# A fused three-block kernel: the end of the weight fold reordered, and the expert rows cleared earlier in the transfer queue

## The reference, cut to what matters

```python
x = x + xattn(layernorm(x), ctx)     # latent cross-attention to 257 context rows, 16 heads
x = x + attn(layernorm(x))           # 4-bit-coded weights w = codes * scales, 16 heads of 128
x = x + ffn(layernorm(x))            # 64 experts, top 8 of each token, capacity 128

q_big  = einsum('bshk,hkq->bshq', hidden @ Wq.T, w_kc_q)
kv_rope = kv * cos + rotate_half(kv) * sin
scores = einsum('bhsr,bhlr->bhsl', q_big @ W_qr, kv_rope @ W_kr)
out    = (softmax(scores) @ kv_rope @ w_kc_kv) @ Wo.T
```

## Time and profile before

| | us |
|---|---|
| median of three runs (lowest, highest) | 736.1 (734.83, 737.74) |
| the profiled execution | 734.79 |
| its span, first to last instruction | 733.0 |
| PE busy | 631.6 (86%) |
| DVE busy | 446.3 (61%) |
| ACT busy | 285.6 (39%) |
| POOL busy | 275.1 (38%) |
| fold | to about 84 |
| tile 0, tile 1 | about 84 to 132, about 132 to 187 |

### The profile page before, as it was taken

How to read it: one execution, slowest core, us unless ns; L and a number is a source line. 1 busy time by engine, 2 the same in 40 slices (tenths; PEclk the granted TensorE clock), 3 DMA queues, 4 the chain that set the end, 5 groups by cost and what they waited for, 6 DMA issues and landing times.

```text
span 733.0 us, 16840 instructions
## 1 busy us (share of the span) xinstructions
PE 631.6 (86%) x6395; PEld 540.9 (74%) x6395; DVE 446.3 (61%) x1257; ACT 285.6 (39%) x788; POOL 275.1 (38%) x296
## 2 busy tenths in 40 slices
PE   5998687989989999999999999998886899999900
PEld 3887556977887896896897896896765688778800
DVE  1143696555677577677677677576573245555548
ACT  1112485336337337337347337346030043333300
POOL 3852599211212612612612612403103435555520
PEclk9556798999999999999999999999999999999965
DMA  7697551990400600500500200100002769998467
GB/s 192 191 250 185 164 190 35 293 325 4 138 2 2 199 2 9 193 2 10 192 3 10 77 3 10 56 3 31 32 4 86 203 196 334 330 318 277 131 254 296
DMA packets 90383, 95.85 MB, mean 131 GB/s; under 512 B 26047, under 2 KB 82104, under 8 KB 89280
## 3 DMA queue, kind: packets, MB, share of 16 engines
q1 hardware_dynamic: 83552, 78.40, 35.8%
q0 software_dynamic: 6144, 15.96, 6.0%
q10 hardware_dynamic: 608, 0.42, 0.2%
HBM read 60.19 MB, written 36.18 MB: 131 GB/s over the span
## 4 chain that ended last, share of the span: by engine, by line
PE 52%; DVE 17%; issue 11%; ACT 8%; DMA 4%; SPq 4%; POOL 2%; another core or an unknown queue 1%; POOLq 0%; DVEq 0%; ACTq 0%
PE bank L1258 6%; PE bank L1259 6%; PE bank L1260 6%; PE bank L1324 4%; PE bank L1292 3%; PE bank L1373 3%; PE bank L1278 3%; PE bank L1543 3%; PE bank L1313 3%; DMA Wh<-expert_rows 2%; POOL pair_rows L650 2%; ACT diag L735 2%; PE bank L1511 2%; ACT qspace L676 2%; DVE space L1212 2%
## 5 line engine op out<-in xcount | busy, mean ns | idle before, releaser
L697 ACT ACTIVATE pr<-bank,nmax 128x257 f32<-128x257 f32 x128 | 61.4, 480 | 95.5 <-DVE nmax L921 92.5
L574 POOL DMA_INDIRECT expert_rows<-h,slot x64 | 63.0, 984 | 69.4 <-DVE slot L1018 53.7
L1258 PE MATMUL bank<-space,Wh 128*128 128x128 f16 x512 | 88.1, 219 | 0.3
L1260 PE MATMUL bank<-space,Wl 128*128 128x128 f16 x512 | 88.1, 219 | 0.0
L1259 PE MATMUL bank<-space,Wh 128*128 128x128 f16 x512 | 88.1, 219 | 0.0
L557 POOL TENSOR_TENSOR Cr<-C,Ct 128x192 f32<-128x192 f32 x64 | 39.3, 636 | 122.4 <-PE bank L1324 113.3
L650 POOL DMA_INDIRECT pair_rows<-Wh,etok x64 | 62.4, 974 | 56.5 <-issue 36.2
L921 DVE TENSOR_REDUCE nmax<-bank 128x1 f32<-128x257 f32 x128 | 53.4, 421 | 43.0 <-PE bank L1306 30.1
L705 ACT COPY pT<-bank 128x256 f32<-128x256 f32 x128 | 47.6, 372 | 64.1 <-PE bank L1313 61.5
L1324 PE MATMUL bank<-Cr,pT 128*128 128x64 f32 x512 | 72.2, 264 | 0.1
L1324 PEld LDWEIGHTS bank<-Cr,pT 128*128 128x128 f32 x512 | 68.2, 194 | 0.2 <-ACT pT L705 0.2
(11 more groups left out here) (208 smaller groups left out, 1548.2 us busy)
## 6 DMA issues: line engine op xcount, KB each, us to landing
expert_rows<-h SPq DMA_DIRECT2D x8, 1120.0 KB, 13.3
Wh<-expert_rows SPq DMA_DIRECT2D x64, 140.0 KB
pair_rows<-zrow SPq DMA_DIRECT2D x8, 1024.0 KB
Wl<-L_ffn_gate_up_proj_dram SPq DMA_DIRECT2D x36, 192.0 KB
ring<-L_ffn_gate_up_proj_dram SPq DMA_DIRECT2D x28, 192.0 KB
space<-pair_rows SPq DMA_DIRECT2D x5, 1024.0 KB, 9.2
Wl<-L_ffn_down_proj_dram SPq DMA_DIRECT2D x36, 96.0 KB
C<-ctx_dram SPq DMA_DIRECT2D x24, 128.0 KB
```

The source lines that it names most:

```text
L574: e.indirect_dma_start(XE[:, :], bass.IndirectOffsetOnAxis(ap=slot[:, k:k + 1], axis=0), h3[:, :], None, bounds_check=E * CAP - 1, oob_is_ ...
L697: e.activation(pr[:, s, :], bank[r % 2][:, 0:NL], ACT.Exp, bias=nmax[:, s:s + 1], accum_out=rsum[:, s:s + 1]).then_inc(expd, 1)
L1258: e.matmul(dst, ah, bh, start=first and n == 0, stop=False)
L1260: ins = e.matmul(dst, al, bh, start=False, stop=last and n == len(terms) - 1)
```

## The change

`FOLD_PARTS` goes from (0, 0, 2, 3) to (0, 0, 1, 4): part 0 alone stays in the third group, and parts 1 to 4 are given to the fourth. Part 4's multiply and cast are done in tile 0 at r = 1. DVE takes part 1 ahead of `kt0`'s low half, part 2 ahead of `qa`'s, part 3 behind `fQ`, and the split of the value bias ahead of the last `M` copy. PE makes `qb` at r = 2 of tile 0, so behind the first two score rows. POOL does the rope products of tile 1 in the fold, between the low halves of parts 0 and 1, and SP loads context 1 ahead of part 1. SP issues the eight `blank` transfers ahead of the wait for all parts; transfer n waits for `expd` 6 + 2n, that is for 6, 8, ... 20 rows.

```diff
-FOLD_PARTS = (0, 0, 2, 3)
+FOLD_PARTS = (0, 0, 1, 4)
@@ SP
             load_fold_first(3)
+            e.wait_ge(roped, 2 * BT)
+            load_context(1)
             load_part(1)
...
                 load_codes(LATE + n, late[n], late_in[n])
-            e.wait_ge(roped, 2 * BT)
-            load_context(1)
-
             e.wait_ge(f_m, GROUPS)
...
             load_codes(PARTS - 1, late[10], late_in[10])
-            e.wait_ge(w_done, PARTS)
...
+            e.wait_ge(iotas, 2)
+            for n in range(E // 8):
+                e.wait_ge(expd, 6 + 2 * n)
+                blank(n)
+
+            e.wait_ge(w_done, PARTS)
             for n in range(NB):
                 load_expert(n, n)
             for i in range(2, T):
                 e.wait_ge(roped, i * (2 * BT))
                 load_context(i)
-                if i == 2:
-                    e.wait_ge(iotas, 2)
-                    for n in range(E // 8):
-                        blank(n)
@@ POOL
-            for u in range(PART0[GROUPS]):
+            part_low(0)
+            rope_products(1)
+            for u in range(1, PART0[GROUPS]):
                 part_low(u)
...
-                if not last:
+                if not last and i != 0:
                     rope_products(i + 1)
@@ ACT, in tile 0 behind exp_row; and in the fold
+                        if isinstance(i, int) and i == 0 and r == 1:
+                            x_use(XNEXT[-1], 0)
+                            part_high(LATE - 1)
...
-                for u in range(PART0[g], PART0[g + 1]):
+                for u in range(PART0[g], min(PART0[g + 1], LATE - 1)):
                     part_high(u)
-
-            x_use(XNEXT[-1], 0)
@@ DVE, in tile 0 behind max_row; and in the fold
+                        if isinstance(i, int) and i == 0 and r == 1:
+                            part_mul(LATE - 1)
+                            x_low(XNEXT[-1], 0)
...
                 if g == GROUPS - 1:
-                    for name in XNEXT[1:-1]:
-                        x_low(name, 0)
-                if len(left) > 2:
                     part_mul(left.pop(0))
+                    x_low("kt0", 0)
+                    part_mul(left.pop(0))
+                    x_low("qa", 0)
@@ PE, in tile 0 ahead of score_row
+                        if isinstance(i, int) and i == 0 and r == 2:
+                            e.wait_ge(f_md, GROUPS)
+                            e.wait_ge(f_na, GROUPS)
+                            x_use("qb", 0)
                         if r < ROWS:
                             score_row(i, r)
...
-            e.wait_ge(f_md, GROUPS)
-            e.wait_ge(f_na, GROUPS)
-            x_use("qb", 0)
             tile(0, None, None)
```

More of the change, by code:

```diff
@@ L1146, in _ @@
                     part_mul(left.pop(0))
+                if g == GROUPS - 1:
+                    e.wait_ge(rwT_ready, 3)
+                    e.tensor_copy(bvh[:, :], bvT[:, :]).then_inc(bv_split, 1)
+                    e.wait_ge(bv_split, 1)
+                    e.tensor_tensor(bvl[:, :], bvT[:, :], bvh[:, :], ALU.subtract).then_inc(bv_split, 1)
                 e.wait_ge(f_m, g + 1)
@@ L1152, in _ @@
                     next_h1(0)
-                for u in left:
-                    part_mul(u)
-            x_low(XNEXT[-1], 0)
+                if g < GROUPS - 1:
+                    for u in left:
+                        part_mul(u)
             e.sem_inc(h3_free, FREE)
             e.wait_ge(iotas, 2)
[L1160 to L1163, removed]
             tile(0, None, None)
```

## The result

The changed kernel takes 746.58 us (median of 4 runs) against 735.47 us for the kernel before, 11.1 us more, a ratio of 1.0152 with a 95% interval of 1.0102 to 1.0203. On a second chip it was 1.0201 (1.0160 to 1.0241), 741.04 us against 727.94. The forecast was 745.8, slower. The profiled execution took 746.07, with a span of 744.3, which is 11.3 more than the span before.

What follows compares the result with a forecast made beforehand. PE carries half the chain and fills tile 1, though no engine holds it everywhere. +0.7 + 11.8 + 2.0 - 4.8 = +9.7 on 734.8 gave 744.5, or 745.8 as median; range 740.5 to 752.

Steps and rivals of the forecast that it cites:

- The context behind the clearing: Tile 1, SP's queue: context 2 waits behind clearing transfers 6 and 7 and 16 expert issues, reaching POOL at 154.7.
- DVE's wait and PE's loss: Tile 1: DVE stands from 145.9 to 159.2, PE loses 11.8 us, and its lowered clock adds 2.0.
- What may come back: Middle of tile 1: PE's unexplained wait and the low clock behind it vanish, -4.8 us; the other end is 0.
- The 3.14: PE's wait in us before 163.89 in tile 1, with no releaser, read as a late instruction refill behind clearing traffic.
- the rival at 750.5: Tile 1: the 3.14 stays, or a like one comes to tile 0; +14.5, 750.6 us; chance 0.28.
- The fold's end: Up to row 2 of tile 0: waiting for part 4's load replaces the shortened path, +0.7 us (+0.1 to +1.5).
- my bracket for row 2: Tile 0: score row 2 starts at 88.7, between 88.1 and 89.5, by the landing of part 4's scales.
- no wait: Fold, DVE: part 3, landed by 75.8, is multiplied at about 76 without waiting.
- The bias split: Fold, DVE: its two small operations move into the wait for M, hidden, and 0.4 us at most otherwise.

Runs made afterwards that it cites:

- context_ahead_of_last_two: The changed kernel with context 2 loaded between the sixth and seventh clearing transfers; 735.36 us against 738.17 for the kernel before, 0.9984.
- clearing_and_context_alone: The kernel before, old fold, with clearing ahead of the wait for all parts and context 2 between its sixth and seventh transfers; 733.72 us against 736.82, 0.9951.
- clearing_only: The kernel before with only the eight clearing transfers moved ahead of the wait for all parts, with their row waits; 753.6 us against 738.17, 1.018.
- order_only: The changed kernel with the clearing put back behind context 2, where it was before; 739.05 us against 738.17 for the kernel before, 1.0011.

## Why the prediction was right

The direction, the mechanism and its place were right. The sum was near, +9.7 forecast and +11.1 measured on the first chip, but that nearness is partly luck: the stages add up to +13.4, as worked out below, and the second chip had +13.1. The steps, by the stages:

*The context behind the clearing: right, with terms that partly cancel.* The gate opened at 137.2, 6.5 behind the first maximum of tile 1, as before. The last clearing transfer issued in 0.36 where I had 0.75. The 16 expert transfers took 11.07 (137.75 to 148.82) where I had 8.82. That is the term I sized too low: I took the issue time ahead of the clearing, and here two clearing transfers were still in front, with the first four issues at 0.56 to 1.31 and a later one at 1.35. The other kernels bear it out: the 16 issues took 7.7 to 9.0 in the three that issue them ahead of the clearing, and 10.8 to 12.5 in the eight that issue them right behind two clearing transfers. The landing was quicker, 3.06 behind the last issue (150.35 to 153.41) instead of 3.78. Altogether POOL had the context 22.7 behind the first maximum of tile 1, and I had 21.4 (154.7 less 133.3).

*DVE's wait and PE's loss.* DVE waited 14.5 where I had 13.3, and PE 11.9 where its loss was to be 11.8 in all. With the half clock that followed the stage grew from 53.2 to 68.2, 15.0; I had 11.8 + 2.0 = 13.8. PE's clock came back in some 5 us, as in the earlier trace rows.

*What may come back: the size right, its nature not shown.* The 3.14 was a wait under the clearing traffic, and it went also in the kernels where PE has no long pause that could hide it (context_ahead_of_last_two, 0.5 at that matmul). With its clock it is worth 57.6 - 53.2 = 4.4; I had 4.8. That it is a fetch of instructions I infer from "issue" and the traffic; what the runs show is that the wait needs the clearing's traffic at that matmul. Here the Trainium skill's page "Runtime: NRT & Kernel Launch", section "Instruction fetch mechanics", with its "mostly hidden", was the rival at 750.5 (750.6 by the forecast's own terms). It didn't come about. The page does say "mostly", and of all waits without a releaser that PE has in tile 1 only this one followed the traffic.

*The fold's end: the place right, the size too small.* I said that a wait for part 4's load would take the place of the path that was shortened, at +0.7. That wait is 4.42, 4.45, 6.14 and 3.32 in four of the five traces with the changed kernel's fold; in the fifth, context_ahead_of_last_two, it is 0.59, and `qb` is the later one. With full clock row 2 stands 29.5, 29.4, 30.4 and 28.5 behind the third M copy in the new order, mean 29.4, and 26.5 and 26.6 in the old: +2.8. With half clock it is 30.8 against 29.1 and 29.4: +1.6. By the same mark my bracket for row 2, 88.1 to 89.5, was 26.6 to 28.0. That row 2 started at 86.07, ahead of the bracket, is due to the early third M copy alone. `part_low(1)` took 2.93 instead of 2.12, and the last scales were in DVE's hands 6.0 behind their issue at 77.4, where the longest landing in the earlier trace rows was 5.4. The codes of parts 5 and 6 were issued right behind them. I didn't test which of these it was. Part 3, for which I had written "no wait", waited 1.04 for its scales, and 0.78 to 1.98 in the other four.

*The bias split: wrong, and without effect in the changed kernel.* I called it hidden, 0.4 at most. It took 4.13 and held M's copy, and with it `qb`, by about 4 us. It cost nothing in the end only because part 4 was later still, at 83.36, while `qb` had been cast at 83.1. In context_ahead_of_last_two, where part 4 came sooner, it was on the path. There part 4's multiply was done at 87.44 and `qb`'s low halves began at 90.03, so an estimate of its cost from these two is 2.6.

Summed anew, with the fold at full clock as in the two profiles compared: +2.8 + 15.0 - 4.4 = +13.4, 1.8% of 735, between the two chips' ratios. The forecast's terms were +0.7, +13.8 and -4.8.

What stays open is the spread of whole executions: the same kernel differs by 5 to 10 us through the fold's clock and the stages behind tile 2, and I looked for no cause of it.

## What to carry to other kernels

When a transfer is given a wait of its own in a hand-written queue, write down everything behind it and who needs that; the cheap transfer with the late consumer must not stand ahead of the urgent one. A gate counted in rows has to be checked against the rows of a tile: 6 + 2n passes 16 at the seventh transfer (n = 6), and that, with the expert weights and the context queued behind it, turned a gain of 0.5% (clearing_and_context_alone) into a loss of 1.8% (clearing_only). And where whole executions spread by more than the effect, compare stages between marks, not ends, and only traces that had the same clock in the stage.

## What the runs showed of the hardware

Tiny DVE operations can take as long as the POOL operation beside them. The split's two operations on 128x16 elements took 2.09 and 2.04 us in the changed kernel, and 0.17 and 0.18 in order_only. POOL's timeline of the changed kernel shows a subtraction running at each of those times:

```profile
72.64 2.93 POOL L588 TENSOR_TENSOR Wl<-ring,Wh 128x1024 f16<-128x1024 f32 x1 [2.97 <-ACT Wh L666]
75.54 2.11 POOL L588 TENSOR_TENSOR Wl<-diag,Wh 128x1024 f16<-128x1024 f32 x1
77.61 2.12 POOL L588 TENSOR_TENSOR Wl<-ring,Wh 128x1024 f16<-128x1024 f32 x1
```

POOL's first subtraction took 2.93 instead of 2.1; `part_mul(3)` ran on DVE until 73.59 beside it. The ends match: 73.51 + 2.09 = 75.60 against 75.57, and 75.64 + 2.04 = 77.68 against 77.65. The Trainium skill's page "SBUF — State Buffer", section "SBUF: two separate sides", has the rule: a port pair shared by the two engines is held for a whole instruction, and the loser is fully blocked. It limits this to DVE instructions in certain fast modes or with two inputs in SBUF. This trace agrees, with both numbers above, and with M's copy, whose source is a bank of PSUM: it took its usual 0.68 from 77.61 on, while POOL subtracted from 77.61 to 79.73.

A transfer's issue on SP is no fixed price: 16 expert transfers took 8.82 us ahead of the clearing and 11.07 behind two clearing transfers, and a clearing transfer 0.36 when each waited for its own rows, and 3.03 (median) when all eight were issued in a row.
